# Slots four times finer in a planned attention and feed-forward pipeline, and an ending of its own for the last batch

## What is computed

```python
scores = jnp.einsum('bhsd,bhtd->bhst', q, q) / jnp.sqrt(jnp.float32(E))
same = (b_hs[:, :, :, None] == b_hs[:, :, None, :]).astype(scores.dtype)
attn = jax.nn.softmax(scores * (NB - 2 + same), axis=-1)
out = jnp.einsum('bhst,bhtd->bhsd', attn, v)
...
h = jax.nn.silu(_tlin(x, w1_w, w1_s)) * _tlin(x, w2_w, w2_s)
h = jax.nn.gelu(_tlin(h, h1_w, h1_s), approximate=False)
h = jax.nn.gelu(_tlin(h, h2_w, h2_s), approximate=False)
return _tlin(h, w3_w, w3_s)
...
x = x + _layernorm(_L0_attn_ref(_layernorm(x, axis=-1), ...), axis=-1)
x = x + _layernorm(_L0_ffn_ref(_layernorm(x, axis=-1), ...), axis=-1)
```

## Time and profile before

| what | value |
|---|---|
| time, median of 3 runs | 1357.16 us (1356.61 to 1359.28) |
| the profiled execution's own time | 1353.54 us |
| its span, first to last instruction | 1351.7 us |
| busy, PE / DVE / POOL / ACT | 1229.4 / 1202.0 / 1187.1 / 1105.2 us |
| share of the span, PE / DVE / POOL / ACT | 91% / 89% / 88% / 82% |

### The profile page before, as it was taken

One profiled execution on the slowest core, in us unless ns is written; L12 is line 12 of the kernel. 1 busy time (PEld: TensorE's weight loads), 2 busy tenths in 40 slices (PEclk: granted clock), 3 DMA queues, 4 the chain that ended last, 5 costly groups with the idle time before them and its releaser, 6 DMA issues. The chain is left out here.

```text
span 1351.7 us, 19878 instructions
## 1 busy us (share of the span) xinstructions
PE 1229.4 (91%) x5315; PEld 507.9 (38%) x5406; DVE 1202.0 (89%) x3790; ACT 1105.2 (82%) x1701; POOL 1187.1 (88%) x309
## 2 busy tenths in 40 slices
PE   4676799999999999999999999999999999999987
PEld 1221244334344434434343433434443443433343
DVE  4999999999999999999999999999999999999420
ACT  2355788989897988989898898989889898979875
POOL 2599989899989989998998999999999999999900
PEclk9877899999999999999999999999999999999999
DMA  3474445534544454464445434454454445443100
GB/s 90 139 204 124 132 113 150 135 120 129 157 110 126 134 138 133 114 157 123 135 113 152 134 116 139 124 148 126 124 149 125 139 121 149 121 124 106 53 8 8
DMA packets 89189, 167.13 MB, mean 124 GB/s; under 512 B 18034, under 2 KB 54004, under 8 KB 89076
## 3 DMA queue, kind: packets, MB, share of 16 engines
q1 hardware_dynamic: 88968, 165.56, 44.1%
q10 hardware_dynamic: 108, 0.30, 0.1%
HBM read 150.33 MB, written 15.47 MB: 123 GB/s over the span
## 5 line engine op out<-in xcount | busy, mean ns | idle before, releaser
L983 POOL TENSOR_TENSOR logits<-max_row,logits 128x2048 f32<-128x2048 f32 x256 | 1156.8, 4557 | 80.9 <-DMA max_row<-max_scratch 80.3
L839 DVE CUSTOM_DVE_ANT_0 logits<-s_bank,coeff 128x512 f32<-128x512 f32 x1024 | 692.1, 676 | 0.0
L1037 ACT ACTIVATE logits<-logits 128x1024 f32<-128x1024 f32 x512 | 507.5, 1047 | 80.0 <-POOL logits L983 79.1
L789 DVE TENSOR_SCALAR coeff<-brow,bcol 128x516 bf16<-128x516 bf16 x1024 | 486.6, 475 | 48.0 <-PE s_bank L571 27.5
L571 PE MATMUL s_bank<-mov_stack,stat_stack 128*128 128x512 bf16 x933 | 319.9, 393 | 48.9 <-DVE rowmax L839 39.5
L593 PE MATMUL aux_bank<-logits,v_pad 128*32 128x512 f32 x2048 | 251.9, 611 | 1.1 <-ACT logits L1037 0.6
L728 PE MATMUL f_bank<-hid_b,h_sb 128*128 128x512 f32 x512 | 249.3, 594 | 2.8 <-ACT hid_b L1193 1.3
L717 PE MATMUL f_bank<-hid_a,h_sb 128*128 128x512 f32 x512 | 250.4, 595 | 0.1
L571 PEld LDWEIGHTS s_bank<-mov_stack,stat_stack 128*128 128x128 bf16 x1024 | 95.8, 99 | 325.2 <-DVE rowmax L839 209.3
L728 PEld LDWEIGHTS f_bank<-hid_b,h_sb 128*128 128x128 f32 x512 | 95.3, 190 | 91.7 <-issue 71.1
L717 PEld LDWEIGHTS f_bank<-hid_a,h_sb 128*128 128x128 f32 x512 | 95.0, 190 | 81.1 <-issue 69.7
(11 more groups left out here) (120 smaller groups left out, 914.7 us busy)
## 6 DMA issues: line engine op xcount, KB each, us to landing
max_row<-max_scratch SPq DMA_DIRECT2D x128, 512.0 KB, 3.9
brow<-bucket_scratch SPq DMA_DIRECT2D x63, 522.0 KB, 6.7
mov_stack<-q_scratch SPq DMA_DIRECT2D x192, 96.0 KB
stat_stack<-q_scratch SPq DMA_DIRECT2D x189, 96.0 KB
max_scratch<-rowmax_T SPq DMA_DIRECT2D x512, 1.0 KB
q_scratch<-q_parts SPq DMA_DIRECT2D x16, 384.0 KB, 2.6
x_in<-in_x SPq DMA_DIRECT2D x16, 256.0 KB, 3.0
q_scratch<-q_parts SPq DMA_DIRECT2D x16, 256.0 KB, 3.0
```

What stands on the lines that cost most here:

```text
L789: nc.vector.tensor_scalar(coeff[:, k % 3, :].rearrange("p (r n) -> p r n", r=ROW_RUNS), brow[:, h // 4 % 2, h % 4, :, 0:RUN], bcol[:, b % ...
L839: nc.vector.tensor_tensor_reduce(out=logits[:, ring(b, k), :], in0=tile_bank(k)[:], in1=coeff[:, k % 3, 0:SEQ], scale=float(E) ** -0.5, sc ...
L983: nc.gpsimd.tensor_tensor(tiles[:, :, t:t + 2], max_row[:, m % 2].unsqueeze(2).broadcast_to([P, GROUP, 2, SEQ]), tiles[:, :, t:t + 2], ALU ...
L1037: nc.scalar.activation(logits[:, first:first + 2, :], logits[:, first:first + 2, :], ACT.Exp, scale=-1.0).then_inc(probs_done, 1)
```

## The change

All slots of PE, DVE and ACT become quarters of a tile (`STEPS_PER_TILE = 4`, 256 steps for an iteration); those of SP and POOL stay in tiles. The numbers are new too, not only multiplied by four, and the value sums, copies, transposes, divisions and exponentials get tables of their own in place of one lag. Work and sizes of the steady part stay.

Iterations 16 and 17 are replaced by a `finale` on each engine, written out by hand. Groups 6 and 7 of batch 15 are subtracted by DVE (L1085, L1091) in place of POOL. Batch 15's layer uses the score banks and free tiles of the `logits` ring (`last_hid_a`, `last_hid_b`), so its matmuls stand between those of batch 14's layer. Its first hidden layer runs over the inner index outside. The last output is scaled and added by DVE and stored in four parts, one for each row block.

```diff
+STEPS_PER_TILE = 4
+STEPS = TILES * STEPS_PER_TILE
...
-GATE_SLOTS = (43, 45, 47, 48)
-UP_SLOTS = (47, 51, 52, 53)
+GATE_SLOTS = (180, 180, 198, 200)
+UP_SLOTS = (185, 205, 209, 216)
...
-OUTPUT_SLOTS = (100, 102, 104, 106)
+OUTPUT_SLOTS = (402, 406, 413, 415)
...
-YNT_SLOT = 42
-YNT_COPY_SLOT = 38
+YNT_SLOT = 161
+YNT_COPY_SLOT = 170
...
-                for k in range(TILES):
-                    if attend:
-                        scores(i, k)
+                for k in range(STEPS):
+                    if attend and k % STEPS_PER_TILE == 0:
+                        scores(i, k // STEPS_PER_TILE)
...
+            def finale():
+                first, second, third = FIRST_HIDDEN_SLOTS[-1] + 1, SECOND_HIDDEN_SLOTS[2], SECOND_HIDDEN_SLOTS[3 * HT]
+                for slot in range(STEPS, first):
+                    ffn_step(LAST - 1, slot, True)
+                for j in range(ST):
+                    weigh_values(LAST, QUADS - 2, j, False, False)
+                for slot in range(first, second):
+                    ffn_step(LAST - 1, slot, True)
+                weigh_last_values()
+                transpose_output(LAST, PAIRS - 1)
+                for slot in range(second, third):
+                    ffn_step(LAST - 1, slot, True)
+                last_gates()
+                for slot in range(third, OUTPUT_SLOTS[0]):
+                    ffn_step(LAST - 1, slot, True)
+                last_ups()
+                last_first_hidden(0)
+                for slot in range(OUTPUT_SLOTS[0], 2 * STEPS):
+                    ffn_step(LAST - 1, slot, True)
+                for k in range(1, HT):
+                    last_first_hidden(k)
+                last_layers()
...
+                for h in range(GROUP):
+                    one = logits[:, first + h * ST:first + (h + 1) * ST, :]
+                    nc.vector.tensor_tensor(one, max_row[:, m % 2, h:h + 1].broadcast_to([P, ST, SEQ]), one,
+                                            ALU.subtract).then_inc(last_below_max_done, 1)
...
+                for t in range(ST):
+                    dve.wait_ge(end_rstd_done, LAST + t + 1)
+                    nc.vector.scalar_tensor_tensor(out=ffn[:, t, :], in0=last_out_bank[t][:, 0:E], scalar=end_rstd[:, t:t + 1],
+                                                   in1=y1[:, LAST % 2, t, :], op0=ALU.mult,
+                                                   op1=ALU.add).then_inc(last_out_done, 1)
...
+                for t in range(ST):
+                    sp.wait_ge(last_out_done, t + 1)
+                    sp.dma_start(out_view[LAST][:, t, :], ffn[:, t, :]).then_inc(out_stored, 16)
```

More of the change, by code:

```diff
@@ new lines, in last_gates @@
+            def last_gates():
+                for t in range(ST):
+                    pe.wait_ge(last_yn_done, t + 1)
+                    last = nc.tensor.transpose(s_bank[2][:, t * P:(t + 1) * P], x_res[:, t, :], ident[:])
+                last.then_inc(ynT_psum, 1)
+                pe.wait_ge(ynT_done, LAST + 1)
+                for j in range(HT):
+                    if j == 3:
+                        pe.wait_ge(y1_done, LAST + 1)
+                    nc.tensor.matmul(s_bank[j][:], w1_sb[:, j * P:(j + 1) * P], ynT[:], start=True, stop=True).then_inc(w1_psum, 1)
@@ L778, in _ @@
+            stages(pe, iteration, finale)
         @block.vector
@@ L1042, in rstd @@
                 act.wait_ge(ready, count)
-                nc.scalar.activation(log[:], var, ACT.Ln, bias=eps[:], scale=scale).then_inc(log_done, 1)
+                nc.scalar.activation(log, var, ACT.Ln, bias=eps[:], scale=scale).then_inc(log_done, 1)
                 act.wait_ge(log_done, n)
-                nc.scalar.activation(out_[:], log[:], ACT.Exp, scale=-0.5).then_inc(done, 1)
+                nc.scalar.activation(out_, log, ACT.Exp, scale=-0.5).then_inc(done, 1)
             def scale_rows(dst, src, rstd_, rstd_done, n, done):
@@ L1138, in att_scale @@
             def att_scale(f):
-                if f:
+                if f and f < LAST:
                     act.wait_ge(h2_done, (f - 1) * HT + 2)
```

426 lines of the change are left out of this document (294 added, 132 removed).

## The result

The changed kernel takes 1332.78 us, the median of 4 runs (1330.96 to 1335.87), against 1356.88 us of before measured beside it (4 runs, 1355.36 to 1359.28): a ratio of 0.9826, 95% interval 0.9803 to 0.9850. The forecast was 1328. The profiled execution took 1333.48 us, with a span of 1331.7 in place of 1351.7.

What follows compares the result with a forecast made beforehand. No engine alone bounds a steady batch, where engines wait for each other; PE bounds the end. Steady 22 plus end 7 gave 29 us off 1357.16: 1328 us, range 1316 to 1343, for all cases 1313 to 1352.

Steps and rivals of the forecast that it cites:

- Steady part: Full iterations 2 to 13 win 18.6 us, batches 14 and 15 together 3.4: 22 us from idle time removed.
- I take half of DVE's idle time, 1.55 us for a batch: Steady batches: of DVE's 3.10 us idle a batch, half goes, since three near-full engines don't run without gaps.
- the four waits: PE's waits on ACT for `ynT`, gelu, silu and the attention's copy: 22.6 of PE's 31.4 us idle in nine batches.
- `ynT`: PE's gates wait for ACT's copy; five tiles of scores ahead in place of one should remove all 8.1 us.
- Gelu ahead of the output: PE's output waits for ACT's gelu; sixteen value-sum matmuls and a tile of scores as cover should remove 6.3 us.
- Silu and the attention's copy: PE's ups and transposes move back one to one and three quarter tiles; their 8.2 us of waits go in good part.
- The end: After DVE's last tile, DVE's subtractions, shorter PE waits and output in parts win 7 us, between 0 and 10.
- The waits only change their place: Rival: the ACT waits go but DVE still meets PE's dense pieces; only the end is won, 1350 us; chance 0.13.
- All goes: Rival: DVE never waits in the steady part, 43.9 us, with the end 51: 1306 us; chance 0.10.
- A product too early on DVE: Rival: the second product waits for its up matmul, up to 2.7 us a batch, giving 1366 us; chance 0.10.
- A slow end: Rival: DVE's SBUF subtractions take POOL's 4.5 us, so the end gives nothing: 1335 us; chance 0.08.
- The first two I count at nothing: The first two batches, before the full iterations 2 to 13, were taken to win no time.

Runs made afterwards that it cites:

- x12_act_less: Changed kernel with the four exponentials of one of four groups of heads on only 256 of their 512 columns, nothing moved: 1318.99 us.
- x8_gates_only: Old slots times four with the new ending, only gates, ups, silu, products and `ynT` transposes and copy at new slots: 1356.68 us, 1.0009 of before.
- x1_old_steady: Changed kernel with every steady slot four times the old one, so the new ending alone: 1346.03 us, 0.9931 of before.
- x2_old_end: Changed kernel with iterations 16 and 17 as before in place of the finale, so the new slots alone: 1342.96 us, 0.9917 of before.
- x11_pool_tail: Changed kernel with POOL, not DVE, subtracting groups 6 and 7 in the ending: 1340.49 us.
- x4_pool_less: Changed kernel with POOL subtracting only the first 384 of 512 columns of each tile and the exponential's scale at -0.001: 1325.22 us.
- x7_spread: Changed kernel with the first matmul of the hidden layer moved from step 216 to 220, behind the next scores: 1332.54 us.

## Why the prediction came out as it did

**Sign and size** were right: 24.1 us between the medians where I had forecast 29. It is a sum of a term twice too large and one somewhat too small, so that the total came this close is in part luck: the two traces differ by only 20.0.

**Steady part, 22 us forecast, 10.8 measured.** The step that was mis-sized is "I take half of DVE's idle time, 1.55 us for a batch": it was 3.10 - 2.32 = 0.78. The nine batches give 6.7 us, batches 14 and 15 together 2.2 where I had 3.4. The reasoning behind it failed at "the 8.2 us should go in good part" and at the start, "the worth is the idle time that it removes". I took the four waits as four covers that were too short, each of which a longer cover would mend. They were faces of one full queue, and only the wait for gelu went whole. The 22.6 us of the earlier trace rows became 9.6, but 13.5 us of new waits for ACT came up. The prediction said that these three engines can't run without gaps; it left out the fourth, ACT, whose mean is 82%. The table by a stretch of half a batch shows it, and the trace of before had that row (33.94 of 34.30). That this queue bounds the base period was shown, for the changed kernel, by taking work out of it (x12_act_less); for the kernel before it rests on that row.

- *`ynT`*: "The 8.1 us should go": 3.5 are left, and 4.5 now stand one step earlier, where the transposes wait for `x_res` (L690). The cause that I gave, five tiles of scores in place of one, isn't enough: x8_gates_only has them, and waits 16.3.
- *Gelu ahead of the output*: 6.3 us forecast to go, 0.0 left (L766). Here the longer cover did what was said.
- *Silu and the attention's copy*: 8.2 became 6.1.
- The longer batches I hadn't seen as a term of their own. Of the 0.75 us that a batch won on the mean (77.73 to 76.99), 0.34 are the base period (76.97 to 76.63), and 0.41 that the mean lies nearer to it: 0.76 us above before, 0.36 now. Only the first is sure. The second varies from trace to trace with the same slots: 0.50 in x1_old_steady with the old, 0.26 (x2_old_end) to 0.53 (x11_pool_tail) with the new. What is left of it goes when POOL has less to do (x4_pool_less); that POOL made it in the kernel before too was not tested.

**The end, 7 us forecast, 9.2 measured.** Row by row: the subtraction "2.3 us for 2048", measured 2.25; PE's waits 0.6 + 1.0 + 0.7 = 2.3, measured 0.93 + 1.34 + 0.68 = 2.95; from DVE's last tile to the span's end 80, measured 1331.7 - 1253.43 = 78.3. The rest is PE's work, which I had at 73.6 us and which is 71.41 up to 1328.00, and an ending behind PE of 1331.7 - 1327.87 = 3.8 us, where I had 4.3. I didn't find why PE's busy time is 2 us shorter; no run took that apart. By parts, I had 3.8 us for PE's path and 3.5 for what stands behind it, and they gave 5.2 and 4.0. The first needs the new order and DVE's subtraction together (x11_pool_tail).

**The rivals.** *The waits only change their place* (1350) was half right: they did, but the time still fell by half of the term. *All goes* didn't. *A product too early on DVE*: L1007 waits 3.4 us in nine batches, 0.38 a batch, where the rival needed 2.1. *A slow end*: no, 2.25 us.

**What I had counted at nothing.** "The first two I count at nothing": between the first and the second mark 79.10 us became 76.64, 2.5 us of the 10.8. It repeats: 80.85 in x1_old_steady with the old slots, 76.61 in x2_old_end with the new. The start up to the first mark took 101.54 us before and 102.61 after; traces with the new slots have 101.69 (x7_spread) to 102.70 (x11_pool_tail), so no cost of the start is shown.

**The two rules of the Trainium skill.** The lock between a DVE instruction with two SBUF inputs and a GpSimd instruction that reads SBUF (the Trainium skill, SBUF — State Buffer, Who interferes with whom): this trace has an overlap of 0.15 us. POOL's last residual begins at 1253.11 and takes 1.31, DVE's subtraction begins at 1254.27 and takes 2.30, the next, without an overlap, 2.28. Nothing of the lock is seen in that, but so short an overlap is no test; the end was built so that the two don't meet. The drain with a table load (the Trainium skill, ScalarE: Activation LUTs, What ACT_TABLE_LOAD costs): nothing is seen of it either, since the load at 617.76 is followed by its silu at 619.05, 1.29 us later.

**Left open.** Which of the moved slots shortened the base period from 76.97 to 76.63, since PE's waits for ACT kept their sum. What takes the other 0.3 of each us that x12_act_less freed, and which other chain then sets 75.55 us. How the 5.2 us of PE's path at the end divide between the order and DVE's subtraction. That the six table loads in the full stretch, 6 x 1.28 = 7.7 of its 34.3 us, would give as much as exponentials do if silu and gelu shared a load is an estimate from these rows; it wasn't tried.

## What to carry to other kernels

A busy share of 82% over a kernel can be a queue that is full for half of each batch. Where several waits name the same engine, take them as one sum: cut the period into stretches of a quarter or half and see if that engine is full in one. If it is, moving its work around may win little (here 0, and a loss of 19 us, in two tries; the whole new table 0.34 us of the base period), and the test is to take some out and see whether the period follows.

A step that moves out of a full queue comes back as a wait of whoever used it last, and may even cost more, when it had filled a wait. Longer single waits of PE can also bring a lower clock with them, so read the granted clock of an experiment before its loss is put down to the order alone. When a table of slots is retuned, its numbers work together: a part of it alone cost 10.7 us, the whole won 11 to 13.

At an end without new work, look for the slowest engine in the chain behind the last input and give its work to one that has run dry. In the new order that was worth 8.4 us, 3.3 of it by the clock that PE then kept. Count the part behind the last matmul by itself: by the rows, to let the last output leave in pieces, without POOL, was worth 4.0 of the 9.2 us.
